# A GRU scan with a ternary feed-forward: step 0's loads, the last half of W_hh, the quantisation and the closing sums are moved

## The reference

```python
gi = x @ W_ih + b_ih;  gh = h @ W_hh + b_hh          # 256 -> 3 * 256
r = sigmoid(i_r + h_r); z = sigmoid(i_z + h_z); n = tanh(i_n + r * h_n)
h_new = (1 - z) * n + z * h

# ternary_quant, in bf16, groups of 64 weights
scale = mean(|w|);  q = clip(round(w / scale), -1, 1);  w_hat = q * scale

gate, up = split(h @ wq_gu.T)                        # 256 -> 2 * 1024
hid = silu(gate) * up;  hn = hid * rsqrt(mean(hid * hid) + eps)
out = x + hn @ wq_p.T                                # 1024 -> 256
```

## Time and profile before

| | |
|---|---|
| median of 3 runs | 358.7 us (358.64 to 358.98) |
| the profiled execution | 358.56 us |
| its span, first to last instruction | 356.7 us |
| PE busy | 345.1 us, 97% of the span |
| DVE, ACT, POOL busy | 227.9, 212.2, 171.4 us |
| mean granted clock of TensorE | 0.999 |

### The profile page before, as it was taken

One profiled execution on the slowest core, in us unless ns is written; L12 is line 12 of the kernel. 1 busy time (PEld: TensorE's weight loads), 2 busy tenths in 40 slices (PEclk: granted clock), 3 DMA queues, 4 the chain that ended last, 5 costly groups with the idle time before them and its releaser, 6 DMA issues.

```text
span 356.7 us, 5439 instructions
## 1 busy us (share of the span) xinstructions
PE 345.1 (97%) x2031; PEld 298.6 (84%) x2031; DVE 227.9 (64%) x433; ACT 212.2 (59%) x406; POOL 171.4 (48%) x144
## 2 busy tenths in 40 slices
PE   7899999899899999999999999999999999999995
PEld 3789897688788888888898888888888888898884
DVE  7688886978648454765547545775656546644643
ACT  4776676776736666366556556466565556655650
POOL 1022121166444448355363456445462556789881
PEclk9999999999999999999999999999999999999999
DMA  7990000017001000040001000010001000010101
GB/s 244 366 416 6 2 1 2 0 44 310 1 2 59 0 3 1 30 148 1 2 0 61 0 0 2 0 62 1 2 0 59 2 0 2 1 59 2 59 3 59
DMA packets 5570, 17.92 MB, mean 50 GB/s; under 512 B 420, under 2 KB 2084, under 8 KB 5032
## 3 DMA queue, kind: packets, MB, share of 16 engines
q1 hardware_dynamic: 5544, 17.58, 13.0%
HBM read 13.38 MB, written 4.19 MB: 49 GB/s over the span
## 4 chain that ended last, share of the span: by engine, by line
PE 75%; DVE 11%; ACT 6%; issue 4%; DMA 2%; SPq 1%; POOL 0%; POOLq 0%; DVEq 0%
PE ps_ffn L734 26%; PE ps_out L769 15%; PE ps_rz L665 6%; PE ps_rz L666 6%; PE ps_rz L670 6%; PE ps_n L665 3%; PE ps_n L666 3%; PE ps_n L670 3%; PE ps_t L727 2%; DMA x_ring<-in_L_ffn_w_gate_up_dram 2%; PE ps_rz L734 2%; PE ps_t L780 2%; DVE work L502 1%; DVE q_keep L543 1%; DVE o_st L541 1%
## 5 line engine op out<-in xcount | busy, mean ns | idle before, releaser
L277 POOL TENSOR_TENSOR hid_lo<-work,hid_hi 128x512 fp32r<-128x512 f32 x63 | 82.5, 1310 | 117.2 <-ACT hid_hi L344 117.2
L734 PE MATMUL ps_ffn<-st_hi,wguT 128*128 128x512 f32 x240 | 95.1, 396 | 1.9 <-DVE work L502 1.9
L734 PE MATMUL ps_ffn<-st_lo,wguT 128*128 128x512 f32 x240 | 94.2, 392 | 0.0
L284 POOL TENSOR_TENSOR sq_sum<-sq_sum,work 128x512 f32<-128x512 f32 x54 | 71.8, 1330 | 0.0
L502 DVE TENSOR_TENSOR work<-work,ps_ffn 128x512 f32<-128x512 f32 x56 | 38.4, 685 | 37.6 <-ACT work L340 36.8
L734 PEld LDWEIGHTS ps_ffn<-st_hi,wguT 128*128 128x128 f32 x240 | 45.1, 188 | 11.2 <-DVE work L502 3.6
L734 PEld LDWEIGHTS ps_ffn<-st_lo,wguT 128*128 128x128 f32 x240 | 45.1, 188 | 7.5
L512 DVE TENSOR_TENSOR work<-work,ps_ffn 128x512 f32<-128x512 f32 x64 | 43.9, 686 | 8.5 <-PE ps_ffn L734 6.9
L344 ACT CAST hid_hi<-work 128x512 fp32r<-128x512 f32 x63 | 38.8, 615 | 13.9 <-DVE work L512 13.9
L769 PEld LDWEIGHTS ps_out<-wpT,hid_hi 128*128 128x128 f32 x256 | 37.8, 189 | 4.6 <-DVE o_st L527 1.0
L340 ACT ACTIVATE work<-ps_ffn 128x512 f32<-128x512 f32 x56 | 32.9, 588 | 14.3 <-PE ps_ffn L734 14.2
(11 more groups left out here) (143 smaller groups left out, 667.7 us busy)
## 6 DMA issues: line engine op xcount, KB each, us to landing
out_dram<-o_st SPq DMA_DIRECT2D x7, 512.0 KB, 2.6
xT_all<-in_x_dram SPq DMA_DIRECT2D x1, 3072.0 KB, 17.3
x_ring<-in_x_dram SPq DMA_DIRECT2D x1, 3072.0 KB, 9.8
x_ring<-in_L_ffn_w_gate_up_dram SPq DMA_DIRECT2D x4, 512.0 KB, 9.9
x_ring<-in_L_ffn_w_proj_dram SPq DMA_DIRECT2D x2, 512.0 KB, 10.3
x_ring<-in_x_dram SPq DMA_DIRECT2D x1, 1024.0 KB, 5.7
work<-in_L_cond_W_ih_dram SPq DMA_DIRECT2D x2, 384.0 KB, 3.9
work<-in_L_cond_W_hh_dram SPq DMA_DIRECT2D x2, 384.0 KB, 5.6
```

The lines of the kernel that those rows point to most:

```text
L277: nc.gpsimd.tensor_tensor(hid_lo[:, j % RING], hid[:, j % 2], f32(hid_hi[:, j % RING]), ALU.subtract).then_inc(hid_lo_ok, 1)
L284: nc.gpsimd.tensor_tensor(sq_sum[:], sq_sum[:], hid_sq[:, j % 2], ALU.add).then_inc(sq_added, 1)
L734: mm = pe.matmul(bank, w, group_state(part, G, k), start=(k == 0 and i == 0), stop=(k == KD - 1 and i == 1))
```

## The change

PE's list for the end, with the projection of tile 6 split into its high and its low part ("H6", "L6"), and the loads of the start:

```diff
-PE_END = ["T5", "D6", "T6", "T7", "D7"]
+PE_END = ["T5", "T6", "H6", "T7", "L6", "D7"]
...
-            sp.dma_start(xT_all[:, :, 0:2, :], xt[:, :, 0:2, :]).then_inc(ld_x0, 16)
+            sp.dma_start(xT_all[:, :, 0:1, :], xt[:, :, 0:1, :]).then_inc(ld_x0, 16)
             for k in range(KD):
                 sp.dma_start(wi[:, k], w_ih[k * P:(k + 1) * P, :]).then_inc(ld_wi[k], 16)
+            sp.dma_start(wh[:, 0], w_hh[0:P, :]).then_inc(ld_wh[0], 16)
             sp.dma_start(cT[:], cond_t.rearrange("(k p) b -> p k b", p=P)).then_inc(ld_cT, 16)
-            for k in range(KD):
-                sp.dma_start(wh[:, k], w_hh[k * P:(k + 1) * P, :]).then_inc(ld_wh[k], 16)
+            sp.dma_start(wh[:, 1], w_hh[P:2 * P, :]).then_inc(ld_wh[1], 16)
+            sp.dma_start(xT_all[:, :, 1:2, :], xt[:, :, 1:2, :]).then_inc(ld_x1, 16)
             sp.dma_start(h_nat[:, 1, :], cond).then_inc(ld_c, 16)
             load_unit(0)
-            sp.dma_start(xT_all[:, :, 2:LEAD, :], xt[:, :, 2:LEAD, :]).then_inc(ld_x1, 16)
+            sp.dma_start(xT_all[:, :, 2:LEAD, :], xt[:, :, 2:LEAD, :]).then_inc(ld_x2, 16)
             for u in range(1, NU):
```

ACT: step 0's order, the last half of W_hh in three column blocks, the bias tile in two parts, and the quantisation's `q_abs_of` and `q_weights` in other steps:

```diff
+            act.wait_ge(ld_wh[0], 16)
+            nc.scalar.copy(wh_hi[:, 0], wh[:, 0]).then_inc(wh_hi_ok, 1)
             act.wait_ge(ld_cT, 16)
             nc.scalar.copy(state(st_hi, -1), cT[:]).then_inc(h_hi, 1)
-            for k in range(KD):
-                act.wait_ge(ld_wh[k], 16)
-                nc.scalar.copy(wh_hi[:, k], wh[:, k]).then_inc(wh_hi_ok, 1)
-            input_hi(1)
-            q_abs_of(0)
-
-            def bias_tile():
-                act.wait_ge(biased, 1)
-                nc.scalar.copy(bias[:, 0, :], ps_ffn[:, 1, :]).then_inc(bias_ok, 1)
-                nc.scalar.copy(bias[:, 1, :], ps_t[:]).then_inc(bias_ok, 1)
+            act.wait_ge(ld_wh[1], 16)
+            for cols in (R, N, Z):
+                nc.scalar.copy(wh_hi[:, 1, cols], wh[:, 1, cols]).then_inc(wh_hi_ok, 1)
+
+            def bias_tile(i):
+                act.wait_ge(biased, i + 1)
+                nc.scalar.copy(bias[:, i, :], ps_ffn[:, 1, :]).then_inc(bias_ok, 1)
...
                 elif u:
                     q_means(u)
                 else:
-                    bias_tile()
+                    act.wait_ge(ld_x1, 16)
+                    input_hi(1)
                 z_gate(t)
                 n_gate(t)
-                if odd:
-                    q_abs_of(u + 1)
-                elif u:
+                if t == 1 or not odd:
+                    q_abs_of(u + 1 if t else 0)
+                else:
                     q_weights(u - 1)
-                else:
-                    q_means(0)
                 state_hi(t)
                 if t == 0:
-                    act.wait_ge(ld_x1, 16)
+                    q_means(0)
+                    act.wait_ge(ld_x2, 16)
                 if t == LEAD - 2:
                     act.wait_ge(ld_xr, 16)
                 input_hi(t + 2)
+                if t in (1, 3):
+                    bias_tile(t // 2)
...
                 if t == LEAD:
+                    q_abs_of(5)
+                if t == LEAD + 1:
                     q_weights(3)
-                if t == LEAD + 1:
+                if t == LEAD + 2:
                     q_weights(4)
                 if t == LEAD + 3:
                     q_weights(5)
...
-                if t == LEAD:
-                    q_signs(4)
-                    q_abs_of(5)
-                if t == LEAD + 1:
-                    q_signs(5)
+                if t in (LEAD, LEAD + 1):
+                    q_signs(t - LEAD + 4)
```

DVE: `ternary` and `signed` are cut into `difference` and `kept`, `quantised` and `signed`. A unit's first half (scales, difference, kept, magnitude) and second half (quantised, signed) are spread otherwise over the steps:

```diff
-            for k in range(KD):
-                dve.wait_ge(wh_hi_ok, k + 1)
-                nc.vector.tensor_tensor(wh_lo[:, k], wh[:, k], f32(wh_hi[:, k]), ALU.subtract).then_inc(wh_ok, 1)
-            input_lo(1)
+            for i, (k, cols) in enumerate(((0, slice(0, G3)), (1, R), (1, N), (1, Z))):
+                dve.wait_ge(wh_hi_ok, i + 1)
+                nc.vector.tensor_tensor(wh_lo[:, k, cols], wh[:, k, cols], f32(wh_hi[:, k, cols]),
+                                        ALU.subtract).then_inc(wh_ok, 1)
             dve.wait_ge(ld_c, 16)
...
                 if odd:
+                    difference(u)
+                elif u:
+                    quantised(u - 1)
+                state_lo(t)
+                if odd:
+                    kept(u)
                     magnitude(u)
                 else:
+                    if u:
+                        signed(u - 1)
                     scales(u)
-                state_lo(t)
-                if odd:
-                    signed(u)
-                else:
-                    ternary(u)
 
...
                 if t == LEAD:
+                    quantised(3)
+                    signed(3)
                     scales(4)
-                    ternary(4)
+                    difference(4)
+                    kept(4)
                     magnitude(4)
+                if t == LEAD + 1:
+                    quantised(4)
                     signed(4)
-                if t == LEAD + 1:
                     scales(5)
-                    ternary(5)
+                    difference(5)
                 if t == LEAD + 2:
+                    kept(5)
                     magnitude(5)
+                    quantised(5)
                     signed(5)
```

`input_lo(1)` moves behind `n_pre` of step 0. In `input_rz` the wait for `xT_lo` moves from ahead of the high passes to behind them, and a wait for `x_hi` stands ahead of them. PE's `first_state` and its quantisation sums:

```diff
+                pe.wait_ge(wh_hi_ok, 1)
+                for part in (hi, lo):
+                    one(part, wh_hi, 0, ps_rz[:], both)
+                    one(part, wh_hi, 0, n_hid, N)
+                pe.wait_ge(wh_ok, 1)
+                one(hi, wh_lo, 0, ps_rz[:], both)
+                one(hi, wh_lo, 0, n_hid, N)
+                for i, (dst, cols) in enumerate(((ps_rz[:, R], R), (n_hid, N))):
+                    pe.wait_ge(wh_hi_ok, i + 2)
+                    one(hi, wh_hi, 1, dst, cols)
+                    one(lo, wh_hi, 1, dst, cols)
+                pe.wait_ge(wh_ok, 2)
+                one(hi, wh_lo, 1, ps_rz[:, R], R, True).then_inc(r_sum, 1)
+                pe.wait_ge(wh_ok, 3)
+                one(hi, wh_lo, 1, n_hid, N, True).then_inc(n_sum, 1)
+                pe.wait_ge(wh_ok, 4)
+                pe.wait_ge(r_ok, 1)
+                one(hi, wh_hi, 1, ps_rz[:, Z], Z)
+                one(lo, wh_hi, 1, ps_rz[:, Z], Z)
+                one(hi, wh_lo, 1, ps_rz[:, Z], Z, True).then_inc(rz_sum, 1)
...
-            bias_rows(ps_ffn[:, 1, :], RZ, True)
-            bias_rows(ps_t[:, 0:D], N_IN, True)
-            bias_rows(ps_t[:, D:2 * D], N_HID, False).then_inc(biased, 1)
+            bias_rows(ps_ffn[:, 1, :], RZ, True).then_inc(biased, 1)
             first_state()
-            q_group_sums(0)
...
                 if t == 0:
-                    pe.wait_ge(bias_ok, 2)
+                    q_group_sums(0)
                 transpose_state(t)
                 input_n(t + 1)
                 if t % 2:
                     q_group_sums((t + 1) // 2)
+                if t == 2:
+                    pe.wait_ge(bias_ok, 1)
+                    bias_rows(ps_ffn[:, 1, 0:D], N_IN, True)
+                    bias_rows(ps_ffn[:, 1, D:2 * D], N_HID, False).then_inc(biased, 1)
...
-                if t == LEAD + 1:
-                    q_group_sums(5)
...
+                if t == LEAD:
+                    q_group_sums(5)
```

## The result

The changed kernel takes 365.36 us (median of 4 runs, 364.8 to 365.57) against 358.67 for the kernel before (4 runs, 358.64 to 358.98): a ratio of 1.0179 [1.0162, 1.0196], so slower by 6.7 us. The forecast was 361.9, and its range ended at 363.6. The profiled execution of after took 365.36 us as well, with a span of 363.6.

What follows compares the result with a forecast made beforehand. PE was taken as the bound from 110 to 330 us, passing earlier losses on whole. Terms -1.1 + 0.0 + 0.1 + 4.5 + 0.1 - 0.3 = +3.3 on 358.56 gave 361.9 us, range 360.3 to 363.6.

Steps and rivals of the forecast that it cites:

- The start: Step 0: earlier r gate brings the transpose at 14.8 instead of 15.88 us; -1.1 us (-0.7 to -1.25).
- Steps 1 to 7: Small DVE gains in odd steps against two extra bias products in step 2; sum 0.0 us (-0.2 to +0.3).
- the 0.05 of odd steps: Odd steps: z limits the gain from shorter DVE work to 0.05 us each, four times, -0.2 us.
- Steps 8 and 9: PE's 1.2 us wait for `q_abs` goes, its wait for `gated` grows instead; 0.1 us (-0.35 to +0.3).
- U4's wait: Step 10: U4 waits for the later weight cast, starting at 84.0 instead of 79.47; +4.5 us (+2.8 to +4.7).
- The lower bound of +2.8: Step 10: with DVE as before, the cast behind the tanh ends at 82.3, so U4 waits 2.8 us.
- Step 10 and 11: Step 10: one more DVE operation (+0.7), tile 4's work done earlier (-0.6); 0.1 us; U4's whole delay passed on.
- rival 1: Clock falls in U4's wait; slow products behind the gap cost about 1.4 us more, total 363.3 us; chance 0.2.
- The end: Last matmuls: T7 ends 0.47 us earlier, output rows start at 352.34 instead of 352.64; -0.3 us (-0.2 to -0.3).
- Rival 2: Step 9: DVE and POOL don't pile up, U4 at 82.3 to 83.4, total 360.2 to 361.3 us; chance 0.12.
- rivals 3: Step 0: the start gives nothing, group sums and load order take back the gain; total 363.0 us; chance 0.05.
- Rival 4: Step 10: the cast is early and U4 hardly waits, so the kernel gets faster, 357.4 us; chance 0.05.

Runs made afterwards that it cites:

- e4: Kernel before with only the new order of PE's last work, including the split halves it needs: 358.44 us, ratio 0.9993.
- e5: Kernel before with only unit 4's weight cast moved on ACT from step 9 to behind step 10's tanh: 361.32 us, ratio 1.0054.
- f3: f1 with step 2's two bias products issued ahead of step 2's transpose instead of behind it: 356.54 us, ratio 0.9937.
- e2: Changed kernel with 18 extra 512-column bias products, their result overwritten, on PE ahead of the first group's U4: 362.7 us, ratio 1.0099.
- e3: Changed kernel with the old order of PE's last work: 365.22 us, ratio 1.0175.
- e6: Changed kernel with the transposed first state loaded ahead of W_hh's first half again, as before: 365.98 us, ratio 1.0206.
- e7: Changed kernel with x of steps 0 and 1 in one load at the head again: 365.36 us, ratio 1.0181.
- f1: Changed kernel with the old end, casts of units 4 and 5 early, DVE quantisation spread into idle places of steps 8 to 10: 356.48 us, ratio 0.9936.
- e1: Changed kernel with unit 4's weights cast on ACT at the end of step 9 instead of behind step 10's tanh: 359.98 us, ratio 1.0031.

## Why the prediction was right about the wait and wrong about what follows it

- **The start (term -1.1): right in size, off in this execution.** Transpose 0 moved by -0.31 in the profiled execution, below the range of -0.7 to -1.25. The path behind the r gate was right: 3.29 us to the transpose (12.28 to 15.57) against 3.25 worked out. The r gate itself, worked out as near 11.5, came at 12.28, because W_ih's second half was cast at 7.54. Over the executions with after's start and loads, transpose 0 comes at 15.57, 14.65, 14.86, 15.08, 15.79, 14.83 and 15.12, a mean of 15.13; with before's start at 15.88, 15.92 and 16.30, a mean of 16.03. So the term measures -0.9 on the whole. What made the load of 7.54 late stays open.
- **Steps 1 to 7 (term 0.0): off by 0.27.** From transpose 0 to transpose 8 it is 44.78 to 44.82 us in before, e4 and e5, and 45.02 to 45.11 in the eight others except f3. f3, which moves two products of 0.23 together off this path and changes nothing else, has 44.81. So it is those two, which the prediction named and wrongly let the 0.05 of odd steps balance.
- **Steps 8 and 9 (term +0.1): right,** at 0.0 up to U2. The wait for `q_abs` became one of 1.65 for `gated`.
- **U4's wait (term +4.5): right to 0.05.** U4 at 83.96 against 84.0, `gated` of tile 3 at 79.81 against 79.86. The reading by which an operation of DVE and one of POOL let each other finish gave `scales` as held up as well, and its row shows 1.52 us instead of 0.42. By the rule of the Trainium skill ("SBUF — State Buffer", "SBUF: two separate sides") DVE's second port pair is locked against GpSimd for a whole instruction, a one-input operation in a fast mode included; the trace agrees. The time of U4 itself, and that of `gated`, fit the forecast because the start and steps 1 to 7 together moved by only -0.05; the delay from U2 to U4 is +4.54, and that is the term. e5 splits it: 1.9 us for ACT's slot, 2.7 for DVE's batch together with unit 3's cast in step 9. The lower bound of +2.8, which took ACT and DVE as before, was 0.9 too high.
- **Step 10 and 11 (term +0.1): this is the step that failed.** The prediction passed "the whole delay" on from U4 at full clock, and set the clock's fall aside as rival 1, with 0.2. It fell, and in every profile of a kernel with this wait except e2's, where the wait is filled. Its price had been put at 1.4 us from the slow products at the start; it is 1.6 (e2 against after) to 1.7 (stations); in e3, e6 and e7, where U4 came at 83.46, 84.20 and 83.90 and the transpose at 89.59, 89.75 and 89.82, the same stretch took 6.13, 5.55 and 5.92 us instead of 3.22, so the price there is 2.9, 2.3 and 2.7. The granted clock says why. It stood at 0.50 for 3.4 us in after (84.4 to 87.8) and in e5 (82.1 to 85.5), and for 6.8 us in e3 (82.7 to 89.6), e6 (82.2 to 89.0) and e7 (82.7 to 89.5), where it fell within the gap already. Half of the part that lies behind U4 is the loss: 3.4 / 2 = 1.7, and 6.1, 4.8 and 5.6 us give 3.1, 2.4 and 2.8. So the price is read from how long the clock stays down with work waiting, and 1.7 is the least that a profiled execution showed behind this wait. The trace before showed no gap over 1.2 us behind the start, so it could not say how long a gap the clock bears; yet 4.5 us was nearly four times the longest that it had borne. The Trainium skill ("TensorE: Matmul & The Clock Gate", "HAM oscillation — how this bites in real kernels") says that the clock drops when PE idles too long between bursts; the trace agrees, and that page should have been given more weight than 0.2. In e5 the clock fell behind a shorter idle time than the page allows for; there the measurement decides.
- **The end (term -0.3): right only with the clock up.** e4 has it at 5.09 instead of 5.39 us, -0.30. After had +0.53, since the clock fell in D7. The term took the clock for granted once more.

Together: -0.31 + 0.26 + 4.54 (between U2 and U4) + 1.72 (U4 to transpose 10) + 0.06 + 0.53 = +6.80, the difference of the two executions (365.36 - 358.56). With the terms as predicted and only the clock's 1.7 us behind U4 added, the sum would have been 363.6. The remaining 1.8 us are the start of this execution (0.8), the two bias products (0.3) and the end (0.8), less 0.1 elsewhere.

Rival 2 (no pile-up) is refuted by `q_signed` and `q_scale`; rivals 3 and 4 by the starts and by U4's wait. Rival 1 is what happened, at a higher price. Rival 4 has something to it in f1: with the cast out of the tanh's way and DVE's batches apart, the change without its new end is faster than before by 2.3 to 2.5 us.

## What to carry to other kernels

When a change opens a gap on PE, price it twice: the gap, and the stretch behind it at half clock, here 4.4 us and 1.7 to 2.9 more. A gap beyond the longest that the traces show at full clock is at risk: here gaps of up to 1.7 us (after, e2) were followed by full clock in every profiled execution, one of 2.3 (e5) was not. Moving background work between steps is decided by slots: from transpose 8 to transpose 11 the same casts and DVE operations cost 6.3 us behind the tanh and in one batch ahead of `gated`, the clock's fall included, and gained 1.6 us spread over idle stretches (f1). A DVE operation that met a POOL operation here took about that one's remaining time on top (`q_signed` 1.67 us instead of 0.68), so count how many POOL operations fall into a batch, not only its own durations.

## What the runs showed of the hardware that had not been expected

- A PE gap of 2.29 us (e5) was followed by a granted clock of 0.50, products 0.43 us apart instead of 0.23, and a loss of 1.7 us, the same as behind a gap of 4.38 us (after). Behind gaps of 4.35 to 4.37 us it was 2.3 to 2.9 us (e3, e6, e7), because the clock stayed at 0.50 for 6.8 us instead of 3.4. In two other executions of e5 the mean clock of 0.998 and the time of 360.1 to 360.4 us speak for no fall.
- The clock also fell without a gap of PE in the listing: in after from 357 us on, behind the 128x1 products of the squares, with PE listed as busy in the whole windows around it. So the listed busy time alone doesn't tell whether the clock will hold. The same code kept its clock in e1, e4 and e7; what decides stays open.
- A bf16 `TENSOR_SCALAR` of 128x1024 (`q_scale`) took 0.43, 0.96 or 1.52 us in after; the longest in step 9 began while `sq_sum` ran on POOL.
- The same list of first loads let W_ih's second half be cast at anything from 6.17 (e1) to 7.74 us (f1). A gain of a few tenths at the start can't be read from one trace.
